# A grouped convolution in Toeplitz form: three products of neighbouring blocks in place of four

## What is computed

```python
# x (32, 64, 1024), cond_128 (32, 128), fside_S_0 (64,), weight (64, 16, 9), c_weight (64, 128)
conv = lax.conv_general_dilated(x, weight, window_strides=(1,), padding=[(4, 4)],
           dimension_numbers=('NCH', 'OIH', 'NCH'), feature_group_count=4)
ctx = einsum('nd,od->no', cond_128, c_weight)
y = conv + ctx[:, :, None] + fside_S_0[None, :, None]
w = kernel.astype(x.dtype) * 2.0 - 1.0               # kernel (1024, 1024), booleans
out = x + scale * einsum('bsi,if->bsf', y, w)        # over the 1024 positions of each row
```

## Time and profile before

| | us |
|---|---|
| median of 3 runs (lowest, highest) | 180.7 (180.5, 181.5) |
| the profiled execution | 180.6 |
| its span, from first to last instruction | 178.8 |
| PE busy (PEld) | 171.2 (147.5) |
| DVE busy | 127.5 |
| ACT busy | 68.1 |
| POOL busy | 7.4 |
| main DMA queue, share of 16 engines over the span | 56.8% |

### The profile page before, as it was taken

One profiled execution on the slowest core, in us unless ns is written; L12 is line 12 of the kernel. 1 busy time (PEld: TensorE's weight loads), 2 busy tenths in 40 slices (PEclk: granted clock), 3 DMA queues, 4 the chain that ended last, 5 costly groups with the idle time before them and its releaser, 6 DMA issues.

```text
span 178.8 us, 2874 instructions
## 1 busy us (share of the span) xinstructions
PE 171.2 (96%) x1010; PEld 147.5 (83%) x1010; DVE 127.5 (71%) x188; ACT 68.1 (38%) x77; POOL 7.4 (4%) x18
## 2 busy tenths in 40 slices
PE   7699999999999999999999999999999999998991
PEld 2379888898989889988989898988998898986781
DVE  5736466979996877687675967596766877587662
ACT  3203993566452543329071634237061502042000
POOL 4230600000000000000000000000000000000000
PEclk9969999999999999999999999999999999999999
DMA  5589697768886792776757793778463650005006
GB/s 216 132 152 279 206 262 188 186 105 207 192 283 164 104 343 47 109 167 125 283 84 175 116 318 56 130 146 204 192 96 55 90 233 0 2 0 235 4 0 235
DMA packets 23629, 27.35 MB, mean 153 GB/s; under 512 B 2752, under 2 KB 19072, under 8 KB 23616
## 3 DMA queue, kind: packets, MB, share of 16 engines
q1 hardware_dynamic: 22176, 25.63, 56.8%
q0 software_dynamic: 368, 1.07, 2.4%
q10 hardware_dynamic: 1072, 0.48, 1.3%
HBM read 10.32 MB, written 8.40 MB: 105 GB/s over the span
## 4 chain that ended last, share of the span: by engine, by line
PE 93%; DMA 2%; DVE 1%; ACTq 1%; issue 0%; DVEq 0%
PE ps_conv L658 33%; PE ps_A L681 28%; PE ps_C L681 14%; PE ps_B L681 7%; DMA taps_nat<-weight 2%; PE ps_B L698 2%; PE ps_A L698 2%; PE ps_toep L698 2%; PE ps_C L698 2%; PE ps_toep L681 1%; PE ps_toep L636 1%; PE ps_C L647 1%; DVE sums L214 1%; PE ps_A L624 1%; DVE x_nat L513 0%
## 5 line engine op out<-in xcount | busy, mean ns | idle before, releaser
L658 PEld LDWEIGHTS ps_conv<-toeplitz,x_blk 128*128 128x128 f32 x512 | 60.4, 194 | 2.6 <-issue 0.8
L658 PE MATMUL ps_conv<-toeplitz,x_blk 128*128 128x128 f32 x512 | 60.8, 278 | 0.0
L475 DVE TENSOR_TENSOR y_sum<-ps_conv,shift 128x512 f32<-128x512 f32 (+1 forms) x33 | 22.2, 674 | 17.4 <-PE ps_conv L658 12.4
L373 ACT CAST hi_S<-sums 128x512 fp32r<-128x512 f32 x28 | 16.6, 620 | 43.4 <-DVE sums L492 42.7
L373 ACT CAST hi_A<-y_sum 128x512 fp32r<-128x512 f32 x24 | 14.0, 616 | 41.5 <-DVE y_sum L475 41.5
L358 ACT COPY x_phase<-x_nat 128x1032 f32<-128x1032 f32 x13 | 28.3, 2177 | 3.0 <-DMA x_nat<-x 3.0
L513 DVE SCALAR_TENSOR_TENSOR x_nat<-ps_A,scale_col,x_nat 128x512 f32<-128x512 f32 x27 | 20.3, 750 | 11.2 <-PE ps_A L681 11.2
L502 DVE TENSOR_TENSOR lo_S<-sums,hi_S 128x512 fp32r<-128x512 f32 x28 | 19.0, 680 | 0.0
L502 DVE TENSOR_TENSOR lo_A<-y_sum,hi_A 128x512 fp32r<-128x512 f32 x24 | 16.3, 682 | 1.7 <-ACT hi_A L373 1.7
L681 PE MATMUL ps_A<-sign_T,hi_S 128*128 128x512 f32 x56 | 16.2, 412 | 1.1 <-DVE x_nat L513 0.9
L681 PE MATMUL ps_A<-sign_T,lo_S 128*128 128x512 f32 x56 | 15.0, 389 | 0.0
(11 more groups left out here) (104 smaller groups left out, 174.3 us busy)
## 6 DMA issues: line engine op xcount, KB each, us to landing
x_nat<-x SPq DMA_DIRECT2D x16, 512.0 KB, 4.2
out<-x_nat SPq DMA_DIRECT2D x15, 512.0 KB, 4.8
x_blk<-x_phase SPq DMA_DIRECT2D x118, 64.5 KB, 2.5
w_bytes<-w_bool SPq DMA_DIRECT2D x2, 512.0 KB, 6.3
shift<-shift_dram POOLq DMA_DIRECT2D x1, 768.0 KB, 6.1
x_blk<-x_phase ACTq DMA_DIRECT2D x6, 64.5 KB, 3.7
x_blk<-x_phase POOLq DMA_DIRECT2D x4, 64.5 KB, 3.0
out<-x_nat SPq DMA_DIRECT2D x1, 256.0 KB, 2.9
```

The lines of the kernel that those rows point to most:

```text
L373: nc.scalar.copy(hi[k][:, :, :], flat(operand(k))).then_inc(hi_ok[k], 1)
L475: nc.vector.tensor_tensor(y_sum[r][:, u, a, :].rearrange("m u a o -> m a u o"), ps_conv[:, a, u, :], shift_of(d, r, a).unsqueeze(2).to_bro ...
L658: now = nc.tensor.matmul(ps_conv[:, a].rearrange("m u o -> m (u o)"), x_blk[r][:, a, s:s + M], toeplitz[:, s, g].rearrange("r u o -> r u ( ...
```

## The change

From double 1 on, the convolution of two neighbouring blocks is done together. With x0, x1, x2 the blocks 2k, 2k+1, 2k+2 and T0, T1 the two Toeplitz matrices, y of the even block is x0 T0 + x1 T1 and that of the odd block x1 T0 + x2 T1. Instead of these four products there are three: m2 = x1 (T0 + T1), m1 = (x0 - x1) T0, m3 = (x1 - x2) T1, with y even = m1 + m2 and y odd = m2 - m3. The 128 weight columns of a product are now 64 even-odd pairs of both images, so a pair of images takes 3 x 4 = 12 products where it took 16.

What is added for it: GpSimd makes x0 - x1 and x1 - x2 (`differences`, two subtractions of 128x512 a pair of images), ACT copies the odd blocks x1 side by side (`odd_blocks`), DVE makes T0 + T1 once, and DVE's additions become three for a pair of images (`add_shift`: m2 plus shift, plus m1, minus m3). The results have image and pair number on the partitions and parity in the free dimension, in `y_two`. Four DMAs of 128 KB for a pair of images, issued on ACT (`to_parity`), carry them to `y_sum` with parity and pair number on the partitions; the rows of the signs are loaded in that order. The convolution of double 0 stays at four products, with 3 x 64 positions copied for each phase in place of 129. ACT's and DVE's splits now take two operands in one instruction (A11 with A12, S1 with S2, S3 with S4). x_nat holds 10 pairs in place of 16, so later loads wait for earlier stores. conv(1, 0) stands after the sixth plain product.

```diff
-EARLY = 8
+EARLY = 4
-CONV_AFTER = {4: 0, 6: 1}
+CONV_AFTER = {5: 0, 6: 1}
...
+SPLITS = {"A": ("A11", "A12"), "S12": ("S1", "S2"), "S34": ("S3", "S4"), "A22": ("A22",)}
...
+        def order(d, r):
+            return 2 * (d - 1) + r
...
         def signs_in(eng, half):
-            eng.dma_start(w_bytes[:, rows, :], w_bool.rearrange("(m p) f -> m p f", p=B)[:, rows, :]).then_inc(w_in[half], 16)
+            for p in range(2):
+                eng.dma_start(w_bytes[p * K:(p + 1) * K, rows, :],
+                              w_bool.rearrange("(k p u) f -> p k u f", p=2, u=B)[p][:, rows, :]).then_inc(w_in[half], 16)
...
             def to_blocks(d, r):
-                sp.wait_ge(conv_done[r], 2 * d)
-                sp.wait_ge(phase_ok[r], B * (d + 1))
+                if d > 1:
+                    sp.wait_ge(dif_ok[r], 2 * (d - 1))
+                    sp.wait_ge(odd_ok[r], d - 1)
+                sp.wait_ge(phase_ok[r], B * d)
...
+            def differences(d, r):
+                if d > 1:
+                    pool.wait_ge(m_done[0], order(d - 1, r) + 1)
+                    pool.wait_ge(m_done[2], order(d - 1, r) + 1)
...
+                pool.wait_ge(blk_in[r], 16 * NG * d)
+                for e in range(2):
+                    nc.gpsimd.tensor_tensor(dif[r][:, e], x_blk[r][:, :, e:e + M:2], x_blk[r][:, :, e + 1:e + 1 + M:2][:, :, 0:K],
+                                            ALU.subtract).then_inc(dif_ok[r], 1)
...
+            def odd_blocks(d, r):
...
+                act.wait_ge(blk_in[r], 16 * NG * d)
+                nc.scalar.copy(odd[r], x_blk[r][:, :, 1:1 + M:2]).then_inc(odd_ok[r], 1)
+
+            def to_parity(d, r):
...
+                for p, made in ((0, y_even_ok), (1, y_odd_ok)):
+                    act.wait_ge(made, order(d, r) + 1)
+                    for i in range(2):
+                        act.dma_start(y_sum[r][p * K:(p + 1) * K, i], y_two[r][i * K:(i + 1) * K, p]).then_inc(y_in[r], 16)
...
             def step(d):
-                for k in ("S3", "S4", "A22"):
-                    high_part(k, d)
+                if runs(d, 2):
+                    odd_blocks(d + 1, 1)
                 if runs(d, 4):
                     to_phases(d + 2, 0)
-                if runs(d, 2):
-                    high_part("A12", d + 1)
-                    high_part("A11", d + 1)
+                high_part("S12", d)
+                high_part("S34", d)
+                high_part("A22", d)
                 if runs(d, 4):
                     to_phases(d + 2, 1)
                 if runs(d, 2):
-                    high_part("S1", d + 1)
-                    high_part("S2", d + 1)
+                    to_parity(d + 1, 0)
+                if runs(d, 4):
+                    odd_blocks(d + 2, 0)
+                if runs(d, 2):
+                    high_part("A", d + 1)
+                    to_parity(d + 1, 1)
...
-                high_part("A21", 0)
+                high_0("A21")
+                odd_blocks(1, 0)
+                odd_blocks(1, 1)
                 to_phases(2, 0)
-                high_part("A12", 1)
-                high_part("A11", 1)
+                to_parity(1, 0)
                 to_phases(2, 1)
-                high_part("S1", 1)
-                high_part("S2", 1)
+                odd_blocks(2, 0)
+                high_part("A", 1)
+                to_parity(1, 1)
...
+            def add_shift(d, r):
...
+                nc.vector.tensor_tensor(uneven, ps_conv[:, 1],
...
+                nc.vector.tensor_tensor(even, ps_conv[:, 0], uneven, ALU.add).then_inc(y_even_ok, 1)
+                dve.wait_ge(m_done[2], n + 1)
+                nc.vector.tensor_tensor(uneven, uneven, ps_conv[:, 2], ALU.subtract).then_inc(y_odd_ok, 1)
...
             def combine(k, d):
...
-                if k in ("S1", "S3"):
-                    dve.wait_ge(y_ok, 8 * d + 8)
+                if k == "S1":
+                    for r in range(2):
+                        dve.wait_ge(y_in[r], 16 * 4 * d)
...
             def step(d):
                 if d > 1:
                     sum_up("C21_A", d - 1)
-                    low_part("S2", d)
+                combine("S1", d)
+                combine("S2", d)
                 sum_up("C11_P2", d)
-                low_part("S1", d)
+                combine("S3", d)
+                combine("S4", d)
                 sum_up("C11_P1", d)
-                low_part("S3", d)
+                low_part("S12", d)
                 if runs(d, 2):
-                    add_shift(d + 1, 0, 0)
...
+                    add_shift(d + 1, 0)
+                sum_up("C12_A", d)
+                low_part("S34", d)
+                sum_up("C22_C", d)
+                low_part("A22", d)
...
             def conv(d, r):
...
+                for m, taps, read in ((1, 2, mid_ok), (0, 0, y_even_ok), (2, 1, y_odd_ok)):
+                    if n:
+                        pe.wait_ge(read, n)
+                    if m == 1:
+                        pe.wait_ge(odd_ok[r], d)
+                    else:
+                        pe.wait_ge(dif_ok[r], 2 * (d - 1) + (1 if m == 0 else 2))
                     for g in range(GROUPS):
...
+                        now = nc.tensor.matmul(ps_conv[:, m, g].rearrange("m u o -> m (u o)"),
+                                               of.rearrange("r b k -> r (b k)"),
+                                               toeplitz[:, taps, g].rearrange("r u o -> r (u o)"), start=True, stop=True)
+                    now.then_inc(m_done[m], 1)
```

More of the change, by code:

```diff
@@ L294, in _ @@
                 step(d)
-            sp.wait_ge(stored, 16 * (PAIRS + 2))
+            for j in range(PAIRS - 1):
+                sp.wait_ge(stored[j], 16)
+            sp.wait_ge(stored[PAIRS - 1], 16 * 3)
         @block.gpsimd
@@ new lines, in to_parity @@
+            def to_parity(d, r):
+                if d == 1:
+                    for k in (("A11", "A12") if r == 0 else ("A21", "A22")):
+                        act.wait_ge(lo_0[k], 1)
+                else:
+                    act.wait_ge(lo_ok["A" if r == 0 else "A22"], d - 1)
+                    for k in (("S2", "S3", "S4") if r == 0 else ("S1", "S3")):
+                        act.wait_ge(s_ok[k], d - 1)
+                for p, made in ((0, y_even_ok), (1, y_odd_ok)):
+                    act.wait_ge(made, order(d, r) + 1)
+                    for i in range(2):
+                        act.dma_start(y_sum[r][p * K:(p + 1) * K, i], y_two[r][i * K:(i + 1) * K, p]).then_inc(y_in[r], 16)
@@ L361, in high_part, with high_0 @@
+            def high_0(k):
+                act.wait_ge(y_0, 3 if k == "A12" else 4 * int(k[1]))
+                nc.scalar.copy(images(hi[k]), operand(k)).then_inc(hi_0[k], 1)
             def high_part(k, d):
-                if k in s_sum:
-                    act.wait_ge(s_ok[k], d)
-                elif d == 0 and k == "A12":
-                    act.wait_ge(y_ok, 3)
+                if k in ("S12", "S34"):
+                    for part in SPLITS[k]:
+                        act.wait_ge(s_ok[part], d)
@@ L367, in high_part @@
                 else:
-                    act.wait_ge(y_ok, 8 * d + 4 * int(k[1]))
+                    act.wait_ge(y_in[0 if k == "A" else 1], 16 * 4 * d)
                 if d > 1:
-                    act.wait_ge(done[PRODUCT_OF[k]], d - 1)
-                elif d == 1 and k not in ("S1", "S2", "S3"):
-                    act.wait_ge(plain_done, LAST_USE["A21" if k == "S4" else k])
-                nc.scalar.copy(hi[k][:, :, :], flat(operand(k))).then_inc(hi_ok[k], 1)
+                    for part in SPLITS[k]:
+                        act.wait_ge(done[PRODUCT_OF[part]], d - 1)
+                else:
+                    act.wait_ge(plain_done, {"A": 6, "S12": 1, "S34": 8, "A22": 4}[k])
@@ L491, in combine @@
                         dve.wait_ge(s_ok[part], d)
[L492 to L493 removed]
+                nc.vector.tensor_tensor(operand(k), operand(left), operand(right), op).then_inc(s_ok[k], 1)
             def low_part(k, d):
[L497 removed]
+                dve.wait_ge(hi_ok[k], d)
                 if d > 1:
[L499 to L502 removed]
+                    for part in SPLITS[k]:
+                        dve.wait_ge(done[PRODUCT_OF[part]], d - 1)
+                else:
+                    dve.wait_ge(plain_done, {"A": 6, "S12": 1, "S34": 8, "A22": 4}[k])
+                nc.vector.tensor_tensor(parts(lo_all, k), group(k), parts(hi_all, k).bitcast(F32), ALU.subtract
                                         ).then_inc(lo_ok[k], 1)
@@ L666, in product @@
             def product(k, d, dest, start, stop, free=None, before=0, c=0, signal=None):
                 of = OPERAND_OF[k]
-                count = d if of in s_ok else d + 1
-                pe.wait_ge(hi_ok[of], count)
+                pe.wait_ge(hi_ok[SPLIT_OF[of]], d)
                 if free and (before or d > 1):
                     pe.wait_ge(summed[free], d - 1 + before)
-                if d == 1 and dest is bank.get(PLAIN_BANK.get(k)):
```

(7 more changed lines are left out.)

328 lines of the change are left out of this document (183 added, 145 removed).

## The result

The changed kernel is slower: 190.95 us in the median (190.4 to 192.2) against 181.0 for the kernel before on the same chip, a ratio of 1.056 (1.050 to 1.062). Forecast was 178.4. The profiled execution took 192.2 us, its span 190.3; it is the slowest of the four.

A forecast was written before the change was run, and what follows sets the result against it. PE work was taken as the bound, busy 171.2 of 178.8 us. Sum: 180.6 - 12.2 (products) + 9.7 (first-double holes) + 0.3 (end) = 178.4 us, y transfers hidden; range 175.5 to 185.5.

The forecast's parts named there:

- Products: PE convolutions from double 1 on: 12 products for 16 save 0.87 us a pair, 12.2 us in all.
- Rival D: PE convolutions: products do not shrink by a quarter, as one alone costs more; chance 0.04, shared with any other case.
- DVE, GpSimd, ACT by load: Each double of 18.1 us: DVE 15.6, GpSimd at most 8.8, ACT about 14 us, so none bounds by load.
- rival B: GpSimd and DVE hinder each other on SBUF operands, giving no gain: 181.3 us; chance 0.12.
- The loop through y: Steady doubles: a round through both pairs' y transfers takes 8.4 + 6i + 2l, hidden under PE's 18.1 us.
- term l: Time from issue to landing of a y transfer: taken at 2.9 us, bounds 2.5 and 4.8.
- 6i + 2l: Six ACT issues (i = 0.55 us) and two y landings: 9.1 us, hidden below 9.7; both upper ends 13.3.
- rival A: Steady doubles: the round through y outlasts PE's 18.1 us, 1.3 us more each, total 187 us; chance 0.20.
- The first double: Load delayed 0.9 us (0.4 to 1.5); PE holes of 7.6 us before P2 of double 1, 2.1 before P6.
- The clock: PE after the first hole: a lower granted clock would cost about 1 us, hidden in the second hole.
- Rival C: First double: the holes do not come, as blocks land sooner or ACT's wait is covered: 168.7 us; chance 0.06.
- 9.7 and 0.3: Losses added to the sum: 9.7 us of PE holes in the first double, 0.3 at the last double's P6.

The follow-up runs named there:

- natural order: Changed kernel with y carried by two 256 KB DMAs a pair in natural block order, signs loaded naturally, 129 positions a phase in double 0: 188.66 us.
- the one at 43.87: Changed kernel without y transfers (results wrong) and with ACT's strided copy for (2,0) ahead of the odd copy of (1,1): 179.9 us, ratio 0.993.
- mended order: Changed kernel with ACT's strided copy for (2,0) moved ahead of the odd copy of (1,1) in the first double: alone 188.82 us, ratio 1.045.
- the three edits together: Changed kernel with natural-order y in two DMAs a pair, loads one double deeper behind y's landing, and ACT's first-double copies swapped: 185.98 us, ratio 1.027.

## Why the prediction was wrong, point by point

- **Products: right.** A convolution of three products takes 2.60 us by the two rows of the changed kernel's PE timeline below, 0.89 less than the 3.49 of the earlier trace rows, and without y's transfers the steady double is 18.2 us; 18.1 was forecast. Rival D is out.

```profile
63.15 2.84 PE L800 MATMUL ps_conv<-toeplitz,w_bytes 128*128 128x128 f32 x24
65.75 1.17 PE L819 MATMUL ps_A<-sign_T,hi 128*128 128x512 f32 x4
```

- **DVE, GpSimd, ACT by load: right in what mattered.** DVE has 15.8 us in the double at 92.00 (15.6 forecast). GpSimd's subtractions are 1.17 to 1.30 us each in the mean, about the lower bound taken (1.3 to 2.2). The experiment without them is no faster, which excludes rival B for the steady doubles.
- **The loop through y: the step that failed.** The mechanism was named; its term l was mis-sized. The landing was taken at 2.9 us, from bounds of 2.5 and 4.8, because the 128 KB stores at the end took 2.8. The forecast calls that one store that stood alone; there are two, issued from 175.0 behind stores of 512 and 256 KB, with no load and no blocks under way, and they landed in 2.5 and 3.1 us. That is the quiet end of the kernel, not the steady double. The last piece of the second pair's y took 4.3 to 6.6 us in those doubles where it was on the path, twice above even the upper bound, and that of the first pair 3.5 to 5.7. In the double from 92.00 the term 6i + 2l, forecast at 9.1 us, is 13.3 (issues 1.8 and 2.0, landings 3.7 and 5.8), the very figure that the forecast gave for both upper ends. The fixed part of the loop was too long: 8.4 us forecast, 6.8 measured (20.17 from S1 to S1 less 13.3). Of the 1.6 us, 0.9 are the cast of A, which is not in the way, since ACT issues a DMA while the cast is still running (issue at 107.20 in a cast that began at 107.07). So l may be 3.8 us in the mean of the two, in place of 3.1. PE's own path from P6 through the second pair, 14.3 + l, allows nearly the same, 3.9. The two paths run level: the profile's chain goes through both pairs' landings, but those of the first pair held the issues of the second by less than 0.1 us at 107.0, by 0.3 and 0.6 at 88.4 and 127.4, and by 2.6 only at 69.2, where the landing took 5.7. A looser bound did not help against a landing that missed it by up to 2.7 us.
- **Why the landing was mis-sized.** The text counted DVE, GpSimd, ACT and PE per double, but not the DMA engines. Their share was 0.63 and y adds 1 MB a double; it came to 0.85. The share was a warning and no measure: with loads and stores moved it stayed at 0.84 to 0.86, and the second pair's landing fell to 2.7 to 3.6 us. What made it long were the load and the two stores issued within 2 us of it: held back until y had landed, they leave its last piece 2.3 to 3.7 us, and a load beside the first pair makes that one 5.2 to 7.6. Block transfers alone still leave up to 5.0. The prediction did see loads in flight (rival A) and priced them at l = 3.7, 1.3 us a double. Measured: 1.9 a double above the 18.2. So rival A happened, at 191 in place of its 187, and a chance of 0.20 was too little for a step with a margin of 0.3 us a transfer and bounds that reached 1.7 beyond it.
- **The first double: mechanism right, size short.** P2 started at 49.50 for 47.3, behind the very chain that was laid out (blocks of (1, 1), strided copy, blocks of (2, 0), odd copy, cast). 0.9 us was taken for the delay of the load that GpSimd waits for; its copy began at 21.92, where it was 18.45 before, so 3.5, beyond the bound of 1.5. By the chain that more than carries the 2.2, but it is not all that holds P2: with natural order the copy began at 18.81 and P2 was only 0.9 us sooner. P6 came 9.7 us after P2 for 8.5: the slow S2 (0.7) and a landing of y of 3.95 at its end are in it. SP's issues and ACT's slow each other where both queues issue: SP's eight block issues from 102.21 took 6.81 us; eight from 94.20, with ACT issuing nothing, took 5.08. The timeline of the changed kernel again, GpSimd's first copy and ACT's odd copy for (2, 0):

```profile
21.92 2.16 POOL L383 COPY x_phase<-x_nat 128x1032 f32<-128x1032 f32 x1 [10.70 <-DMA x_nat<-x]
...
47.84 0.66 ACT L457 COPY set<-x_blk 128x512 f32<-128x512 f32 x1 [4.89 <-DMA x_blk<-x_phase]
```

- **The clock: hidden once, as said, and on the path once.** After the wait of 3.35 us the products at 51.10 and 52.84 run 1.94 and 1.91 us for the usual 1.07 to 1.20. PE is done with them and the convolution at 58.39 (55.55 and 2.84) and still waits for P6 at 59.20, so that costs nothing, as forecast. At 140.39, after a wait of 2.54 us that the forecast did not have, it happens again (2.04 for 1.16), with nothing behind it to hide in: P6 to the next convolution is 5.2 us (140.39 to 145.57) for 3.9 (99.10 to 103.01), 1.3 us. The granted clock is 0.53 from 51.10 to 54.55 and 0.54 from 140.39 to 143.70, the lower level; over the whole of this double, the longest with 22.4 us, it is 0.92.
- **Rival C** did not come: the holes are there in every version, also in the one at 43.87.
- **The sum.** 181.0 less 12.2 for the products gives 168.8. Without y's transfers the time is 182.57, so the first double and what is small beside it take 13.8 us back, where 10.0 (9.7 and 0.3) were forecast; in the profiled execution 11.8 of it stand between the start and P2 of double 2 (69.99 for 58.2). The transfers take 8.4 more, where 0 was forecast: 190.95. The 178.4 and the 190.95 are thus 12.6 us apart: 8.4 for y and about 4 in the first double and beside it, none for the products.

Open: what the first double still loses at 179.9 us once y is gone and the order is mended; why P2 of double 1 starts anywhere from 45.1 to 49.3 us in profiles with the mended order and y carried; why the three edits together take 25.4 us between P2 of doubles 1 and 2 where 22 are usual; and whether another place for y (kept as it is, with the signs and x arranged to suit) would avoid the transfers, which was not tried.

## What to carry to other kernels

Before a change puts a DMA between two steps of a loop, list which loads and stores will be under way when it is issued, and take its landing from transfers that run beside such company, as a maximum over the pieces, since the step waits for the last one. A high busy share of the DMA engines (0.63 before, 0.85 after) says that this needs a look; it does not size the landing, since nearly the same share came with last landings of 2.7 and of 5.8 us. A time read at the quiet end of a kernel, with no loads under way, is a lower bound. When a collision shows, moving the large transfer to another place in the same step can move the collision, as it did twice here; moving it a whole step ahead and behind the landing of the urgent one is what helped. And one profiled execution is no measure of a stretch: the start of double 1 differed by up to 3 us between versions that are the same up to there.

## What the runs showed of the hardware that was not expected

- The same transfer of 128 KB from SBUF to SBUF landed in 2.2 to 6.6 us, by what ran beside it: 2.4 to 2.5 for all four pieces when the last blocks had been issued and no load or store ran, 3.9 to 5.0 for the slowest beside block transfers alone, and 4.3, 5.8 and 6.6 for the last of four with a load and two stores of 512 KB under way.
- ACT starts to issue a DMA while its instruction before is still running (107.07 for 1.05 us, issue at 107.20), so an issue behind a long cast costs less than its 0.62 us.
- GpSimd's two subtractions of 128x512 took 2.06 us in most doubles, 3.03 from 121.95 and 4.64 from 32.35; DVE's low part of 1024 elements took 1.22 us, and 2.07 from 83.39, under subtractions that ran from 82.33.
- Waits of 2.54 and 3.35 us on TensorE were followed by two slow groups of products each (2.04 and 1.65, 1.94 and 1.91 us, for 1.07) at a granted clock of 0.53 to 0.54, the lower of the two levels (1.2 GHz for 2.4), and the wait of 4.51 us in the run without y by three (2.08, 1.91, 1.86). Waits of 1.56 and 2.07 us were not; in the run without subtractions waits of 2.23 and 2.33 us were (2.04 and 1.93).
- Eight block issues on SP took 5.08 us with ACT issuing nothing and 6.81 with ACT issuing y in the same stretch.
